# Three edits to an eight-core transformer layer: the V projection starts before the layer norm has ended, output-projection units are cut in three, and copies out of PSUM move from VectorE to ScalarE

## What is computed

```python
x = x + attn(layernorm(x))
x = x + ffn(layernorm(x))

def attn(x):                     # per batch element: T = 2048, C = 2048
    q = (x @ wq.T + bq).reshape(B, T, 16, 128)
    k = (x @ wk.T + bk).reshape(B, T, 4, 128)
    v = (x @ wv.T + bv).reshape(B, T, 4, 128)
    q, k = rotate(q), rotate(k)
    scores = einsum('btkgd,bskd->bkgts', q, k) * 128 ** -0.5
    p = softmax(scores + tril(ones((T, T))))     # the mask adds 1, it hides nothing
    return einsum('bkgts,bskd->btkgd', p, v).reshape(B, T, C) @ wo.T + bo

def ffn(x):
    return gelu(x @ proj1.T + proj1_bias) @ proj2.T + proj2_bias
```

## Time and profile before

| What | Value |
|---|---|
| median of the runs, with lowest and highest (2 runs) | 3829.56 us (3778.15 to 3880.98) |
| time of the profiled execution | 3739.18 us |
| its span, on the slowest core | 3737.6 us |
| spans of the eight cores | 3712.0 to 3737.6 us |
| mean granted clock of TensorE, by core | 0.949 to 0.954 |
| PE, DVE, ACT busy | 3189.0, 1567.2, 939.9 us |
| stage A to the first V matmul | 0 to 155.7 us |
| V projection on PE | 155.7 to 219.2 us |
| K and Q projection on PE | 221.7 to 498 us |
| attention, first PV to last | 529 to 1648 us |
| tail units | 1650 to 1761 us |
| feed-forward | from 1766 us |

### The profile page before, as it was taken

How to read it: one execution, slowest core, us unless ns; L and a number is a source line. 1 busy time by engine, 2 the same in 40 slices (tenths; PEclk the granted TensorE clock), 3 DMA queues, 4 the chain that set the end, 5 groups by cost and what they waited for, 6 DMA issues and landing times.

```text
span 3737.6 us, 53185 instructions; the slowest of 8 cores (3712.0 to 3737.6 us)
## 1 busy us (share of the span) xinstructions
PE 3189.0 (85%) x20240; PEld 1653.9 (44%) x20240; DVE 1567.2 (42%) x2637; ACT 939.9 (25%) x1747; POOL 95.2 (3%) x178
## 2 busy tenths in 40 slices
PE   4399977788888878874399999999956999999999
PEld 1144445555555555541144444444422444444444
DVE  2412247777777777652413222231323231322223
ACT  3034456644544454430210100101021001010010
POOL 0000000000000000001000000000000000000000
PEclk8699999999999999998699999999987999999999
DMA  6122210033223323338466666666764666566666
GB/s 205 45 57 75 73 29 2 2 97 110 67 75 108 91 58 110 101 77 196 113 156 156 149 153 149 152 151 148 201 184 101 149 152 153 150 151 153 152 158 192
DMA packets 726874, 448.30 MB, mean 120 GB/s; under 512 B 9441, under 2 KB 706145, under 8 KB 724578
## 3 DMA queue, kind: packets, MB, share of 16 engines
q1 hardware_dynamic: 708546, 377.79, 41.4%
q0 software_dynamic: 18080, 67.12, 5.7%
HBM read 411.32 MB, written 33.55 MB: 119 GB/s over the span
## 4 chain that ended last, share of the span: by engine, by line
PE 71%; DVE 10%; DMA 8%; ACT 6%; issue 5%; DVEq 0%; ACTq 0%; SPq 0%; POOLq 0%; POOL 0%
PE pso L994 23%; PE psh L974 21%; PE psqk L384 7%; PE pvps L594 6%; PE wops L530 5%; ACT xn L634 4%; PE ps_t L580 3%; DVE xn L650 3%; DMA p1stg<-p1T 2%; PE sc L570 2%; DMA wstg<-woT 2%; PE psvt L333 2%; DMA xn<-r1T 1%; DMA xstg<-xT 1%; DVE wbf L547 1%
## 5 line engine op out<-in xcount | busy, mean ns | idle before, releaser
L974 PE MATMUL psh<-qbuf,p1bf 128*128 128x512 bf16 x4096 | 889.7, 380 | 78.3 <-DVE p1bf L917 78.3
L994 PE MATMUL pso<-qbuf,p2bf 128*128 128x512 bf16 x4096 | 885.3, 379 | 11.7 <-ACT qbuf L1010 11.7
L634 ACT ACTIVATE xn<-sc 128x896 bf16<-128x896 f32 (+7 forms) x736 | 552.9, 764 | 554.0 <-PE sc L570 501.5
L974 PEld LDWEIGHTS psh<-qbuf,p1bf 128*128 128x128 bf16 x4096 | 401.5, 98 | 565.5 <-issue 85.4
L994 PEld LDWEIGHTS pso<-qbuf,p2bf 128*128 128x128 bf16 x4096 | 400.2, 98 | 496.8 <-issue 15.4
L1010 ACT ACTIVATE qbuf<-psh,b1f 128x1024 bf16<-128x1024 f32 x128 | 142.6, 1114 | 1401.7 <-PE psh L974 1401.6
L917 DVE CAST p1bf<-p1stg 128x2048 bf16<-128x2048 f32 x128 | 156.9, 1227 | 704.6 <-PE psh L974 429.8
L951 DVE CAST p2bf<-p2stg 128x2048 bf16<-128x2048 f32 x128 | 157.0, 1227 | 609.5 <-PE pso L994 528.9
L580 PE MATMUL ps_t<-ident_s,xn 128*128 128x128 bf16 x4096 | 283.6, 225 | 137.4 <-DVE xn L650 137.4
L650 DVE COPY xn<-ps_t 128x2048 bf16<-128x2048 bf16 x256 | 312.0, 1219 | 162.7 <-PE ps_t L580 162.7
L580 PEld LDWEIGHTS ps_t<-ident_s,xn 128*128 128x128 bf16 x4096 | 256.2, 101 | 216.4 <-issue 177.5
(11 more groups left out here) (86 smaller groups left out, 1330.8 us busy)
## 6 DMA issues: line engine op xcount, KB each, us to landing
p1stg<-p1T SPq DMA_DIRECT2D x128, 1024.0 KB, 10.7
p2stg<-p2T SPq DMA_DIRECT2D x128, 1024.0 KB, 7.1
wstg<-woT SPq DMA_DIRECT2D x64, 1024.0 KB, 6.2
wstg<-wqT SPq DMA_DIRECT2D x16, 1024.0 KB, 6.1
xw<-xT POOLq DMA_DIRECT2D x64, 256.0 KB, 3.7
r1T<-r1bw POOLq DMA_DIRECT2D x64, 256.0 KB, 4.3
xstg<-xT SPq DMA_DIRECT2D x8, 1024.0 KB, 5.7
xstg<-xT POOLq DMA_DIRECT2D x8, 1024.0 KB, 5.6
```

Of the source, the lines that this page charges most:

```text
L634: last = s.activation(p_sb[u % 3]()[:, il:ih], sc[sh][:, il - h0:ih - h0], AF.Exp, bias=f32(bias), scale=f32(D ** -0.5), accum_out=acc)
L974: ins = t.matmul(psh[hc % 2][:, sl], p1bf[hc % 2][:, c * 128:(c + 1) * 128], xn2[:, c * TH + ns * SWT: c * TH + (ns + 1) * SWT], start=(c ...
L994: ins = t.matmul(pso2[i % 2][:, sl], p2bf[i % 2][:, hc * 128:(hc + 1) * 128], hblk[:, hc * TH + ns * SWT: hc * TH + (ns + 1) * SWT], start ...
```

## The change

- **V projection.** `full_barrier` gets a parameter `skip`; PE and ACT no longer wait at the barrier ahead of this stage. The weights wv are read twice (two passes over eight token blocks each), now through `wstg` and `wbf` in 8 pieces of four feature chunks, and ACT converts them instead of DVE. PE uses eight PSUM tiles `psvt`, with the chunks of the contraction outside and the token blocks inside, and waits per piece for the four normalised chunks it needs. `wvbf` is gone. ACT evacuates the eight tiles of the first pass between its casts 5 and 6, and those of the second at the end; PE's second pass waits for the first eight.
- **K and Q.** The first cast on DVE now waits for PE's count at the barrier itself; that count has been reached there.
- **Output units.** A unit is emitted as three parts of 6, 5 and 5 matmuls in steps uk, uk+1, uk+2, each behind that step's transposes (and PV). Evacuation and the copy `emit_af` are done by ACT instead of DVE, as activations with the Identity function, behind the exponentials of their step; the evacuation comes in step uk+3 and the addition in uk+4. In the tail DVE emits cast k and addition k-2, and ACT the evacuations.

```diff
-            full_barrier(skip_sync=True)
+            full_barrier(skip_sync=True, skip=("tensor", "scalar"))
...
+                    def phB0_sc(s):
+                        def cast(i):
+                            p.w(s, f"ld_w{i % 2}", 16 * (i // 2 + 1))
+                            if i >= 2:
+                                p.w(s, "s_pe", bB0["s_pe"] + i - 1)
+                            p.inc(s.activation(wbf[i % 2][:, 0:CPS * KVD],
+                                               wstg[i % 2][:, 0:CPS * KVD],
+                                               AF.Identity, bias=f32(0.0)),
+                                  "s_pool")
+
+                        def evac(j):
+                            p.w(s, "s_pe",
+                                bB0["s_pe"] + (j // TPG + 1) * NQP)
+                            p.inc(s.activation(vTb[:, j * KVD:(j + 1) * KVD],
+                                               psvt[j % TPG][:], AF.Identity,
+                                               bias=f32(0.0)), "s_act")
+                        for hv in range(NPASS):
+                            for qq in range(NQP):
+                                cast(hv * NQP + qq)
+                                if qq == 1 and hv >= 1:
+                                    for j in range((hv - 1) * TPG, hv * TPG):
+                                        evac(j)
+                        for j in range((NPASS - 1) * TPG, NPASS * TPG):
+                            evac(j)
...
+                        for g in range(NL):
+                            hv, qq = divmod(g, NQP)
+                            p.w(t, "s_pool", bB0["s_pool"] + g + 1)
+                            p.w(t, "s_dve",
+                                bA["s_dve"] + 5 + 2 * (CPS * qq + CPS - 1))
+                            if qq == 0 and hv > 0:
+                                p.w(t, "s_act", bB0["s_act"] + hv * TPG)
+                            for j in range(hv * TPG, (hv + 1) * TPG):
+                                for ci in range(CPS):
...
-                    if uk <= NU - 2:
-                        pe_at[uk] = k
-                        evac_at[uk + 1] = k
+                    if uk <= NU - 4:
+                        for part in range(3):
+                            pe_at.setdefault(uk + part, []).append((k, part))
+                        evac_at[uk + 3] = k
                         cast_at[uk - 2] = k
-                        radd_at[uk + 2] = k
+                        radd_at[uk + 4] = k
...
-                def emit_unit(t, k):
+                def emit_unit(t, k, part):
                     i, ts = k % NCC, k // NCC
-                    p.w(t, "s_pool", bC["s_pool"] + k + 1)
-                    p.w(t, "s_act_af", af_need(ts))
-                    p.w(t, "s_act", bC["s_act"] + k)
-                    for ca in range(NCC):
+                    if part == 0:
+                        p.w(t, "s_pool", bC["s_pool"] + k + 1)
+                        p.w(t, "s_act_af", af_need(ts))
+                        p.w(t, "s_act", bC["s_act"] + k)
+                    ca0, ca1 = CASPL[part]
+                    for ca in range(ca0, ca1):
...
-                def emit_evac(v, k):
+                def emit_evac(s, k):
                     i = k % NCC
-                    p.w(v, "s_pe", bC["s_pe"] + k + 1)
-                    p.w(v, "s_dve", bC["s_dve"] + max(k - 1, 0))
-                    p.inc(v.tensor_scalar(out=tmpw[k % 2][:], in0=wops[:],
-                                          scalar1=bof[:, i:i + 1], scalar2=None,
-                                          op0=ALU.add), "s_act")
+                    p.w(s, "s_pe", bC["s_pe"] + k + 1)
+                    p.w(s, "s_dve", bC["s_dve"] + max(k - 1, 0))
+                    p.inc(s.activation(tmpw[k % 2][:], wops[:], AF.Identity,
+                                       bias=bof[:, i:i + 1]), "s_act")
...
+                        if u >= 7 and (u - 7) % G == 0 and (u - 7) // G < NKV:
+                            emit_af(s, (u - 7) // G)
+                        if u in evac_at:
+                            emit_evac(s, evac_at[u])
```

More of the change, by code:

```diff
@@ L134, in build_nc, with full_barrier @@
         with nc.Block() as block:
-            def full_barrier(skip_sync=False):
+            def full_barrier(skip_sync=False, skip=()):
                 tgt = {k: v for k, v in p.cnt.items() if v > 0}
-                regs = [block.gpsimd, block.tensor, block.scalar, block.vector]
+                regs = {"gpsimd": block.gpsimd, "tensor": block.tensor,
+                        "scalar": block.scalar, "vector": block.vector}
                 if not skip_sync:
-                    regs.append(block.sync)
-                for reg in regs:
+                    regs["sync"] = block.sync
+                for nm, reg in regs.items():
+                    if nm in skip:
+                        continue
                     def _bar(eng, tgt=tgt):
@@ L339, in build_nc @@
-                    block.tensor(phB0_pe)
-                    def phB0_act(s):
-                        for j in range(NT):
-                            p.w(s, "s_pe", bB0["s_pe"] + j + 1)
-                            p.inc(s.activation(vTb[:, j * KVD:(j + 1) * KVD],
-                                               psvt[j % 2][:], AF.Identity,
-                                               bias=f32(0.0)), "s_act")
-                    block.scalar(phB0_act)
+                    def phB0_sc(s):
[21 more added lines that the diff above has]
+                            evac(j)
@@ new lines, in build_nc @@
+                    block.scalar(phB0_sc)
+                    def phB0_pe(t):
+                        for g in range(NL):
[7 more added lines that the diff above has]
+                                for ci in range(CPS):
+                                    c = qq * CPS + ci
+                                    ins = t.matmul(
+                                        psvt[j % TPG][:],
+                                        xn1[:, c * T + j * 128:
+                                            c * T + (j + 1) * 128],
+                                        wbf[g % 2][:, ci * KVD:(ci + 1) * KVD],
+                                        start=(c == 0), stop=False)
+                            if qq == NQP - 1:
+                                for j in range(hv * TPG, (hv + 1) * TPG):
+                                    ins = t.matmul(psvt[j % TPG][:], ones1[:],
+                                                   bvr_bf[:], start=False,
+                                                   stop=True)
+                            p.inc(ins, "s_pe")
@@ L458, in build_nc @@
                 NUNITS = NTS * NCC
+                CASPL = [(0, 6), (6, 11), (11, NCC)]
                 af_need = lambda ts: (ts + 1) * (SW // 128) * KVH
@@ L613, in emit_af @@
                     src = pvps[:].rearrange("p (g t) -> p g t", t=128)
-                    p.inc(v.tensor_copy(dst, src), "s_act_af")
+                    p.inc(s.activation(dst, src, AF.Identity, bias=f32(0.0)),
+                          "s_act_af")
                 def phC_act(s):
@@ L639, in phC_act @@
                             p.inc(last, "s_act_exp")
+                        if u >= 7 and (u - 7) % G == 0 and (u - 7) // G < NKV:
+                            emit_af(s, (u - 7) // G)
+                        if u in evac_at:
+                            emit_evac(s, evac_at[u])
+                    for kvi in range(((NU - 8) // G) + 1, NKV):
+                        emit_af(s, kvi)
+                    for k in tail_units:
+                        emit_evac(s, k)
                 block.scalar(phC_act)
@@ L680, in phC_dve @@
                                                   op0=ALU.mult), "s_dve_p")
-                        if u >= 7 and (u - 7) % G == 0 and (u - 7) // G < NKV:
-                            emit_af(v, (u - 7) // G)
-                        if u in evac_at:
-                            emit_evac(v, evac_at[u])
                         if u in radd_at:
                             emit_radd(v, radd_at[u])
-                    for kvi in range(((NU - 8) // G) + 1, NKV):
-                        emit_af(v, kvi)
                     tl = tail_units
```

57 lines of the change are left out of this document (21 added, 36 removed).

## The result

The changed kernel takes 3634.6 us as the median of 12 runs (3615.95 to 4024.62), the kernel before 3759.4 us as the median of 10. The ratio is 0.9683, with a 95% interval of 0.9637 to 0.9729: 3.2% faster. Some runs of either kernel were disturbed, the 3880.98 of the two shown ahead among them; they raise the medians, and the ratio leaves them out. The profiled execution of the changed kernel has a span of 3614.7 us on its slowest core, 123 less than before. The mean over the eight cores went from 3724.6 to 3607.4, 117 less.

The account below looks back on a forecast made before the run. In attention, waits of PE and DVE for each other, not either's work, were the limit; PE also idled 72.26 us at V projection. Gains 23 + 14 + 48 + 5 = 90 us give 3649, by the median 3737 (ratio 0.976), range 3660 to 3805.

Parts of the forecast that it names:

- V projection: Ahead of K and Q: PE starts at 110 us instead of idling while DVE normalises; gain 23 us, from 17 to 26.
- the seam: Between the two V projection passes: PE waits 7 us for ACT's cast 6 and eight evacuations.
- Plain steps: Attention without output units: moving the `pvps` copy off DVE makes four steps 14.1 us instead of 14.7; gain 14 us.
- The stretches: Three 52-step attention stretches with output units: 252.5 us each becomes 237, gain 16 each, 48 in all, bounds 27 and 68.
- The series: Computed transpose starts over 12 steps with units and PV: 56.1 us for the kernel before, 53.95 for the changed one.
- so I take half the loss: 237: Stretches: 230 us without clock loss, 243.5 with the same 13.5 loss as now; half the loss gives 237.
- the waits of part 1: A unit's first part waits for ACT's `wops` evacuation, 2.6, 2.0 and 0.3 us in 12 steps, on PE's path.
- Tail: After the last PV: casts for units 49 and 50, and loads behind them, start 7 us earlier; gain 5 us (0 to 8).
- moving the evacuations gives nothing more: Tail: no further gain from evacuating on ACT, since PE must wait for one evacuation on either engine.
- the second rival: Stretches: no loss by the clock at all; whole gain 113 us, so 3626, by the median 3714; chance 11%.
- The clock did not take the gain: First rival: new waits of part 1 keep PE's clock loss in the stretches; gain only 56 us, so 3683; chance 24%.
- Table loads: Third rival: ACT loads a table at each exponential/Identity switch; 68 us slower, 3807; 4%, within 7% for slower.

Follow-up runs that it names:

- the move alone: Attention edits on the kernel before, units left in one piece: evacuation and `pvps` copy go from DVE to ACT behind the exponentials; ratio 0.9808.
- the cut alone: Kernel before with units in three parts, evacuation and `pvps` copy left on DVE; profiled execution 3676.8 us, mean core span 0.984 of the kernel before.
- the earlier casts alone: Kernel before with DVE's casts of the first two tail units ahead of the last `pvps` copy; mean tail 114.5 us.
- The run with longer waits: Changed kernel with two extra 128x512 scratch activations on ACT ahead of each evacuation; profiled execution 3750.9 us.

## Why the prediction was right in its direction and wrong in its size

**V projection: right.** 23 us were forecast, 24.2 measured with that edit alone. Of its steps, the first matmul came at 110.05 (110), the groups every 10.63 (10.6), the seam was 6.05 (7): the eight evacuations took 4.0 together, behind a cast of 1.91, where 5.0 were counted.

```profile
150.94 1.91 ACT L330 ACTIVATE wbf<-wstg 128x2048 bf16<-128x2048 f32 x1 [8.95 <-PE psvt L370]
152.75 4.00 ACT L338 ACTIVATE vTb<-psvt 128x512 bf16<-128x512 f32 x8
```

K and Q started at 194.9 (197). They then ran slower for a moment, as was guessed: from their start to the first PV are 309.4 us, 2 more than before.

**Plain steps: right.** 14.12 us per four, forecast 14.1; 60 steps were 9.5 us shorter, and all the steps between the first and the last PV that lie outside the stretches 14.8 (14).

**The stretches: the mechanism right, the size off.** The series gave 53.95 for 12 steps; patterns without a fall of the clock took 53.98. It also held for the fastest patterns of the variants: 54.2 for the move alone (54.07 to 54.22), 53.4 for the cut alone (53.58), 49.6 with the evacuation first (49.49). The step that failed is "so I take half the loss: 237", the price of the clock. The loss before was put at 13.5 per stretch, and some 7 of it were to stay. The stretches took 229.9, 231.3 and 230.0. Without a fall of the clock the trace gives 228.1: three patterns of 53.98, a last one of 52.0, in which fewer units stand, and 14.1. So the loss that stayed is 1.9, 3.2 and 1.9 us, and the granted clock of 0.99 agrees (1% of 230 is 2.3). The term was forecast at 48 us and came out at 22.6, 22.2 and 22.8, 67.6 in sum, next to its upper bound of 68. About half of it is PE's path (239 to 228, an estimate for before, since there the 239 is the series), where 9 per stretch had been counted, and half the clock, where 7 had been counted.

Why so little of the loss stayed is shown in part. The prediction weighed the waits of part 1 as new chances for a fall. They proved cheap: of the 12 of 2.2 to 2.4 us in the three stretches 4 were followed by the lower level, of the nine of 1.88 none. The 24 waits of 2.3 to 3.3 for the copy of `ps_t`, which the change removes, had been followed by it 15 times. The run with longer waits shows that waits of part 1 can bring the loss back. What decides about a fall is not settled by an experiment; the rows of all kernels, in the last section, say that it is more than the length of a single wait.

**Tail: the size right, the reason wrong.** 5 us were forecast, from an earlier start of the loads. The mean tail of the eight cores went from 116.2 to 109.5, 6.7 shorter, so the size is right. But the V edit alone, with the tail's code as before, had 112.9, and the earlier casts alone 114.5. The reason that was given is not borne out, and the sentence that moving the evacuations gives nothing more is against the runs, in which the short tails go with just that move. The right size was luck.

**The sum.** As means over the eight cores the first PV came 25.5 us earlier, the steps outside the stretches took 14.8 less, the stretches 66.3 and the tail 6.7. That makes 113, and the feed-forward was 3.8 us shorter, which nothing in the change explains. The spans say 117. The forecast was 90; the second rival, no loss by the clock, said 113, and had been given 11%.

**The range.** Two steps put it too high. One is the sum above. The other is the base: the ratio was applied to the median of two runs, 3829.6, though the profiled execution stood at 3739. Five of the ten runs of the kernel before lie between 3728 and 3741, and both of those two lie above them. Against the profiled execution the forecast was 3649 and the second rival 3626. The low end of 3660 took the second rival on the base of 3778 and left nothing for a lower base.

**The rivals.** The clock did not take the gain, though in the run in which the three waits of part 1 were 1.1 to 1.7 us longer the waits and the clock together did: its stretches, 257 to 262 us, are longer than those of the kernel before. Table loads did not come: by the rule cited from the Trainium skill (ScalarE: Activation LUTs, section Table sets: the hidden batching unit), that identity is in every set, none should, and the trace agrees. The rule of the Trainium skill on rotating PSUM banks (Perfetto Trace Analysis, section Matmuls) bore on this change: the waits that come of a single `wops` stood in the series, and they were the largest thing left to gain. No run here has a second bank for it. With one bank still, and the evacuation merely put ahead of the exponentials, the waits went, and 54 us with them.

## What to carry to other kernels

When two engines pass work back and forth through one buffer, neither one's total load gives the time; write down the starts over one full period of the pattern and check the series against the kernel at hand. Here it priced the path of five kernels to 0.2 us in 50, and what the clock took on top, 0.3 to 2 us per pattern in the mean of these, it did not give. Where a copy on a third engine frees a buffer that PE needs next, put it ahead of that engine's long work, at a moment when the engine waits anyway: here this one line gave 54 us, where the two attention edits together gave 83. A base for a forecast is the execution from which its stages are read, not a median of two runs that differ by 100 us.

## What was not expected of the hardware

Short waits of PE are often followed by its lower clock, and two of 1.3 to 1.8 us close together (18 of 24) far more often than one of up to 2.4 that stands alone. Counted are the waits of 1 us or more in the three stretches of each kernel's profiled core, and how often the group behind took over 15% longer than usual. "In pairs" is the second of two waits with only 16 transposes (1.05 us) between them; "alone" has no other such wait in the 7 us ahead:

| Kernel | Waits | Lower clock behind |
|---|---|---|
| before | 24 of 2.3 to 3.3 us, alone | 15 |
| before | 9 of 1.2 to 1.8 | 0 |
| changed | 12 of 2.2 to 2.4, alone | 4 |
| changed | 33 of 1.5 to 1.9, alone | 0 |
| longer waits | 21 of 3.3 to 3.9, alone | 20 |
| longer waits | 12 of 1.3 to 1.45, in pairs | 8 |
| longer waits | 27 others, of 1.3 to 1.9 | 0 |
| cut alone | 12 of 1.6 to 1.8, in pairs | 10 |
| cut alone | 9 of 1.9 to 2.0, alone | 1 |
| cut alone | 33 others, of 1.0 to 1.9 | 1 |
| move alone | 15 of 1.1 to 1.4 | 3 |

Here is such a pair, with the cut alone:

```profile
858.90 1.05 PE L589 MATMUL ps_t<-ident_s,xn 128*128 128x128 bf16 x16 [1.56 <-DVE xn L659]
861.56 2.72 PE L534 MATMUL wops<-qbuf,wbf 128*128 128x512 bf16 x6 [1.60 <-DVE tmpw L549]
```

So the length of the last wait is a poor guide: in the kernel before, waits of 2.6 to 3.3 have no more falls (8 of 14) than those of 2.3 (7 of 10), and the pairs of 1.6 have far more than single waits of 1.9. This comes from comparing kernels that differ in more than this; no run moves two waits apart and leaves the rest alone. One fall costs about 1.6 us of path: 55.6 instead of 54.0 for 12 steps in the changed kernel.
